# First attention of a fused block: queries and keys through memory in rounded parts, scores transposed by the matmul, exp read from PSUM

## The reference, cut to what matters

```python
qh = layernorm(heads(layernorm(x) @ Wq.T + bq), q_gamma, q_beta) * scale   # per head, 16 features
kh = layernorm(heads(ctx @ Wk.T + bk), k_gamma, k_beta)
attn = softmax(einsum('bhqd,bhkd->bhqk', qh, kh))                           # 77 keys
x = x + einsum('bhqk,bhkd->bhqd', attn, vh) @ Wp.T + bp
# next: router logits of layernorm(x), the two best of 8 experts
```

## Time and profile before

| | us |
|---|---|
| median of 3 runs (1414.25 to 1416.54) | 1415.62 |
| the profiled execution | 1416.21 |
| its span | 1414.3 |
| projections | 0 to 110.5 |
| first attention | 110.5 to 371.5 |
| everything behind it | 371.5 to 1414.3 |

### The profile page before, as it was taken

One profiled execution on the slowest core, in us unless ns is written; L12 is line 12 of the kernel. 1 busy time (PEld: TensorE's weight loads), 2 busy tenths in 40 slices (PEclk: granted clock), 3 DMA queues, 4 the chain that ended last, 5 costly groups with the idle time before them and its releaser, 6 DMA issues. The chain is left out here.

```text
span 1414.3 us, 29515 instructions
## 1 busy us (share of the span) xinstructions
PE 1286.1 (91%) x7733; PEld 1026.7 (73%) x7734; DVE 918.5 (65%) x2179; ACT 657.7 (47%) x1386; POOL 715.3 (51%) x903
## 2 busy tenths in 40 slices
PE   7997999999779999999998599857999999859998
PEld 4665777777448888888886477525888888747786
DVE  4784888888656777777776688692333333346665
ACT  2464777777325454544544477454333333221120
POOL 1223566565214655565554466306555555167775
PEclk9998999999799999999999699858999999979999
DMA  3118322222624555555554787535555556664443
GB/s 98 53 37 311 112 86 90 89 82 97 243 101 129 158 157 165 167 156 158 168 163 115 253 234 229 193 149 201 164 162 159 162 162 147 144 212 131 131 132 117
DMA packets 125980, 212.73 MB, mean 150 GB/s; under 512 B 17802, under 2 KB 92571, under 8 KB 122588
## 3 DMA queue, kind: packets, MB, share of 16 engines
q1 hardware_dynamic: 94276, 137.52, 31.5%
q0 software_dynamic: 20640, 56.39, 14.5%
q10 hardware_dynamic: 11000, 18.06, 3.4%
HBM read 148.03 MB, written 59.64 MB: 147 GB/s over the span
## 5 line engine op out<-in xcount | busy, mean ns | idle before, releaser
L1222 POOL DMA_INDIRECT xg<-t_xn,token x160 | 151.7, 948 | 154.6 <-PE psum L2120 70.6
L2196 POOL DMA_INDIRECT su_yg<-t_y,slot x128 | 122.8, 959 | 70.1 <-issue 38.1
L2132 PE MATMUL psum<-gu,m_xT 128*128 x640 | 153.0, 382 | 0.0
L2091 DVE TENSOR_TENSOR m_h<-psum,m_sg 128x256 f32<-128x256 f32 x80 | 33.9, 424 | 157.8 <-ACT m_sg L2070 157.8
L2132 PEld LDWEIGHTS psum<-gu,m_xT 128*128 128x128 f32 x640 | 116.6, 192 | 12.8
L1475 PE MATMUL psum<-w,m_xT_high 128*128 x284 | 119.0, 419 | 0.0
L1497 PE MATMUL psum<-m_both,m_hT_high 128*128 128x512 f32 x284 | 112.5, 418 | 1.4 <-DVE top_i L1441 1.3
L1475 PE MATMUL psum<-w_low,m_xT_high 128*128 x284 | 112.8, 397 | 0.0
L1475 PE MATMUL psum<-w,m_xT_low 128*128 x284 | 112.6, 397 | 0.0
L1348 POOL DMA_INDIRECT t_y<-top_v,dest x36 | 67.8, 1883 | 70.1 <-DVE top_v L1441 69.8
L1422 DVE TENSOR_TENSOR m_both<-w,m_both 128x1024 fp32r<-128x1024 f32 x71 | 87.0, 1225 | 14.1 <-ACT m_both L1390 10.9
(11 more groups left out here) (309 smaller groups left out, 3467.3 us busy)
## 6 DMA issues: line engine op xcount, KB each, us to landing
w<-in_w SPq DMA_DIRECT2D x71, 512.0 KB, 3.8
t_y<-m_y SPq DMA_DIRECT2D x80, 256.0 KB, 2.2
w<-in_w SPq DMA_DIRECT2D x8, 1024.0 KB, 11.3
t_x<-at_x SPq DMA_DIRECT2D x64, 128.0 KB, 2.0
t_w_low<-at_low ACTq DMA_DIRECT2D x64, 128.0 KB, 1.7
w_low<-t_w_low SPq DMA_DIRECT2D x8, 1024.0 KB, 13.3
at_yg<-t_y SPq DMA_DIRECT2D x32, 256.0 KB, 3.3
gu<-in_gu ACTq DMA_DIRECT2D x8, 1024.0 KB, 12.4
```

The lines of the kernel that those rows point to most:

```text
L1222: pool.indirect_dma_start(out=g.xg1[j % GB][:, k * D:(k + 1) * D], out_offset=None, in_=g.xn4, in_offset=bass.IndirectOffsetOnAxis(ap=g.to ...
L2132: last = pe.matmul(ps_gu[p][:, k * 2 * M1:(k + 1) * 2 * M1], xT[p][:, at:at + P], g.gu[:, bass.ds(ex[k] * (DC * 2 * M1) + c * 2 * M1, 2 * ...
L2196: pool.indirect_dma_start(out=yg[p][k][:, :], out_offset=None, in_=g.y1, in_offset=bass.IndirectOffsetOnAxis(ap=g.slot[:, at:at + 1], axis ...
```

## The change

Keys and queries no longer stay in SBUF. `affine` writes each result twice, once in full and once rounded to fp32r (`high`); GpSimd's `part` makes the difference (`low`); SyncE's `store` writes both parts to memory. Before each batch `load_queries_keys` brings them back in nine transfers, as tiles whose rows 0 to 95 are (high, high, low) of the queries and (high, low, high) of the keys, two heads to a tile, the keys in a block for each head. One fp32r matmul over 96 rows then gives the sum of the three products.

```diff
+    def store(self, sp, i):
+        for which, (rows, s_made) in enumerate(((self.high[p], self.s_out), (self.low[p], self.s_low))):
+            sp.wait_ge(s_made, i.n + 1)
+            for first, last in self.store_rows:      # keys: 1, queries: 4
+                sp.dma_start(self.stored[which](i.n, first, last), ...).then_inc(self.st[p], 16)
...
     def affine(self, act, i, s_passed):
+        wait(act, self.s_low, i.shift(-1).n)
+        wait(act, self.st[p], i.div(2).n * self.landed)
         wait_alone(act, self.s_t, i.n + 1, s_passed)
+        for out in (self.full, self.high):
+            last = act.activation(out[p], self.ps_t[:, 0:n], ACT.Identity, bias=self.beta, scale=self.gamma)
...
+def load_queries_keys(sp, g, b, slot):
+    for j, part in enumerate((0, 0, 1)):
+        sp.dma_start(g.q3[slot][32 * j:32 * j + 32, :]..., g.q_parts[part][:, b, :, :]).then_inc(landed, 16)
+    for j, part in enumerate((0, 1, 0)):
+        for a in range(2):
+            sp.dma_start(g.k3[slot][at:at + DH, :]..., g.k_parts[part]...).then_inc(landed, 16)
...
+            def step(s):                              # SyncE, projections
+                if i.within(NQP) and not (i.loop is None and i.off < 4):
+                    load_x(i)
+                if (at := piece(s, OUT + 1)) is not None:
+                    at[0].store(sp, at[1])
+                if s.off in PRELOAD:                  # steps 14, 16, 18, 20: batches 0 to 3
+                    load_queries_keys(sp, g, b, b)
```

```diff
 # TensorE
-                    for a in range(2):
-                        last = pe.matmul(ps_s[:, a, 0:HW], q_s[...], kblk[...])
+                    for i in range(HG // 2):
+                        last = pe.matmul(ps_s[...], g.q3[slot][0:96, ...128...], g.k3[slot][0:96, ...2 * LK...])
+                    for j in range(QUAD):
+                        last = pe.matmul(ps_st[0:LK, ...], g.k3[slot][0:98, ...LK...], g.q3[slot][0:98, ...SQ...])
+                    for a in range(2):
+                        last = pe.matmul(ps_m[:, a * P:(a + 1) * P], mx[...][:, a * HG:(a + 1) * HG], g.ident[:, :])
-                    for h in range(HG):
-                        last = pe.transpose(ps_tp[...], pr[p][:, h * LK:(h + 1) * LK], g.ident[:, :])
 # ScalarE
+                    act.activation(prT[p][0:LK, :]..., ps_st[0:LK, :, :], ACT.Exp)
+                    ln.apply_scalar(act, x1[p][:, :], xn[p][:, :], t)
+                    act.activation(mT[gr][96:96 + HG, :], ps_m, ACT.Copy).then_inc(mt_out, 1)
-                    act.activation(oraw[p][:, :], ps_raw, ACT.Copy).then_inc(raw_out, 1)
 # VectorE
+                    dve.tensor_copy(oraw[b.mod(2)][:, side * 4 * P:(side + 1) * 4 * P], ps_raw).then_inc(raw_out, 1)
-                    ln.apply(dve, x1[p][:, :], xn[p][:, :], t).then_inc(x_norm, 1)
 # SyncE, in this order in a step
+                    sp.wait_ge(mt_out, m.n + 1)       # even steps: two transfers with maxima
+                    expert_weights(e)                 # every eighth step
+                        load_queries_keys(sp, g, nxt.n, nxt.mod(QK_RING))   # every fourth step, until batch 15
+                    input_rows(t)
+                    sp.dma_start(g.w13_low_d[...], low[i.mod(4)][:, :])     # from ScalarE's queue
+                    # x1 and xn out; at step 12 also the 12 transfers for the next phase
-        T_RAW, T_N, T_O, T_WP, T_X, T_R = 4, 5, 6, 7, 9, 10
+        T_ST, T_PV = 5, 6
+        T_RAW, T_N, T_O, T_WP, T_INV, T_AP, T_X, T_R = 10, 12, 14, 15, 16, 17, 19, 20
```

More of the change, by code:

```diff
@@ L174, in __init__ @@
         self.eps, self.ps_p, self.ps_t = eps, ps_p, ps_t
+        n = 2 * DC * rows
+        at = [parts[:, i * n:(i + 1) * n] for i in range(6)]
+        self.full, self.high, self.low = at[0:2], *([a.bitcast(F32R) for a in at[i:i + 2]] for i in (2, 4))
+        self.stored, self.store_rows = stored, store_rows
+        self.landed = 2 * len(store_rows) * 16
         self.sq, self.n = ([sb(f"{name}_{n}{i}", [P, 2 * D]) for i in range(2)] for n in ("sq", "n"))
@@ new lines, in store @@
+    def store(self, sp, i):
+        p = i.mod(2)
+        for which, (rows, s_made) in enumerate(((self.high[p], self.s_out), (self.low[p], self.s_low))):
+            sp.wait_ge(s_made, i.n + 1)
+            for first, last in self.store_rows:
+                sp.dma_start(self.stored[which](i.n, first, last),
+                             rows[first:last, :].bitcast(F32).rearrange("p (c t) -> p c t", c=DC)).then_inc(self.st[p], 16)
+QK_LOADS, QK_RING = 9, 4
+Q_ROWS = [(i * 2 * DH, (i + 1) * 2 * DH) for i in range(P // (2 * DH))]
@@ L329, in _, with step @@
             pool.memset(g.v_all[:, :], 1.0).then_inc(s_v1, 1)
[L331 to L337, removed]
+            for slot in range(QK_RING):
+                pool.memset(g.k3[slot][0:96, :].bitcast(F32), 0.0).then_inc(s_zero, 1)
+            def step(s):
+                if (i := pair(s, X)) is not None:
+                    p = i.mod(2)
+                    wait_alone(pool, ln_mv, i.n + 1, passed[1])
+                    inverse_root(pool, rstd[p][:, :], mv[p][:, :].rearrange("p (a n) -> p a n", a=2)[:, :, 1],
+                                 g.minus_half[:, 0:2], ln_eps, ln_rstd, i)
+                if (at := piece(s, OUT)) is not None:
+                    at[0].part(pool, at[1])
+            steps(pool, FIRST, LAST, TOTAL, BODY, step)
         @block.vector
@@ L607, in _ @@
+            few(TOTAL, half)
             for p in range(2):
@@ new lines, in half @@
+                if v is not None:
+                    b, quad = v.div(4), v.mod(4)
+                    slot = b.mod(QK_RING)
+                    if quad % 2 == 0:
+                        pe.wait_ge(s_mr[quad // 2], (b.n + 1) * 32)
+                    wait(pe, exp_done, v.n)
+                    for j in range(QUAD):
+                        h = 2 * quad + j // 2
+                        last = pe.matmul(ps_st[0:LK, j // 2, j % 2 * SQ:(j % 2 + 1) * SQ],
+                                         g.k3[slot][0:98, (2 * h + j % 2) * LK:(2 * h + j % 2 + 1) * LK],
+                                         g.q3[slot][0:98, h * SQ:(h + 1) * SQ], start=True, stop=True)
+                    last.then_inc(st_mm, 1)
@@ L776, in half @@
+                m = max_rows(u)
+                if m is not None:
+                    pe.wait_ge(mx_ready, m.n * 2 + 2)
+                    wait(pe, mt_out, m.n)
                     for a in range(2):
-                        last = pe.matmul(ps_s[:, a, 0:HW], q_s[p][:, gr * P:(gr + 1) * P],
-                                         kblk[b.mod(2)][:, (2 * gr + a) * HW:(2 * gr + a + 1) * HW],
+                        last = pe.matmul(ps_m[:, a * P:(a + 1) * P], mx[m.mod(2)][:, a * HG:(a + 1) * HG], g.ident[:, :],
```

443 lines of the change are left out of this document (251 added, 192 removed).

## The result

The changed kernel takes 1446.28 us (median of 4 runs, 1435.50 to 1450.47), the kernel before 1416.08 in the same session: ratio 1.0203, 95% interval 1.0141 to 1.0266. It is 2.0% slower, where 1384 was forecast, and lies outside the range of 1360 to 1420. The profiled execution took 1450.25 us, one of the two longest of the four, with a span of 1448.4: projections to 150.5 (40.0 longer), attention to 404.15 (7.35 shorter instead of 63), the rest 1044.25 (1.45 longer).

A forecast was written before the change was run, and what follows sets the result against it. The prediction took TensorE to bound the first attention and SyncE's queue to bind the changed projections. From 1416.2 us it took 63 for the attention, added 30 for the projections and 1.2 for a meeting: 1384, range 1360 to 1420.

The forecast's parts named there:

- The attention: Attention stage: a tile on TensorE costs 5.48 us in place of 7.46, 63 us less over 32 tiles.
- Start and end: Attention outside its steady tiles: 6 us start, 4 stall, 10 last tiles' chain; 20, as the 22 now.
- step 12's stall: Attention, step 12: twelve more transfers pass ahead in SyncE's queue, one stall of about 4 us.
- Maxima scores: Attention: four fp32r matmuls of 154 columns a unit, 0.09 us each, 0.36 a unit; bounds 0.067 and 0.27.
- Transposed scores: Attention: four fp32r matmuls of 256 columns a unit, 4 x 0.112 = 0.45 us.
- Transposed maxima: Attention: two fp32 matmuls of 128 columns, 0.48 us a tile.
- hidden behind TensorE: Projections: ScalarE's second `affine` and GpSimd's difference, 41 and 33 of 48.5 us, add no time.
- Three steps of room: Attention: three steps (8 us) between maxima and transposed scores cover a landing of 1.9, at most 5.4 us.
- A: Attention: short fp32r matmuls run at the fp32 rate, giving 1422 us; chance 0.20.
- C: Projections: the stores hide, ending 3 us later instead of 30, giving 1357 us; chance 0.06.
- D: Attention: the maxima come late every time, 1.9 us for each of 32 tiles, giving 1445 us; chance 0.05.
- B: Attention: SyncE's queue binds there too, 18 us more, giving 1402 us; chance 0.14.

The follow-up runs named there:

- warm_units: Changed kernel plus 4 unread fp32 128x128 products in each of attention units 1 to 14; 1438.34 us.
- warm_proj: Changed kernel plus unread fp32 products in the projections, 5 behind each query pair and 40 at the end; 1448.53 us.
- late_loads: one_store with step 12's twelve loads issued as 17 pieces, one every second step from 14 on; 1433.85 us.
- max_fit: late_max with ScalarE's copy of the transposed outputs moved ahead of its two issues of the maxima; 1405.26 us, ratio to before 0.9929.
- one_store: Changed kernel with each half of a pair's queries stored in one transfer of 128 partitions instead of four of 32; 1426.19 us.
- pause: max_fit with one added TensorE wait, ahead of unit 28's scores, for a residual store to land; 1408.63 us.
- late_max: late_loads with the maxima's two transfers a tile issued by ScalarE instead of SyncE; 1419.70 us, ratio to before 1.0021.

## Why the prediction was wrong

**The clock, the step that failed.** Every duration in "The attention" came from rows at a clock of 1.00, and "Start and end" had 6 us for the start, 4 for the stall and 10 for the last chain. TensorE's idle time did come out at 22.0, in part by luck: 3.2 before step 12's stall, 4.6 for it and 9.0 at the end, and 5.3 in the middle that had been put at nothing. But the 64 units were priced at full clock throughout, and some 39.9 us came from the low one. The rows to ask about were there: 110.50 to 371.50 at 0.96, the end at 0.79. In the kernel before, the stage had 247.88 - 239 = 9 us of it. warm_units and warm_proj show one source, the first units' mix; late_loads and max_fit the other, waits for the maxima, with some 12 us (231.6 - 219.3). The Trainium skill ("TensorE: Matmul & The Clock Gate", HAM oscillation — how this bites in real kernels) tells of waits for a DMA that take the clock down so that its return is paid again each time. late_loads agrees, with prices from some 4 to some 26 us at half clock behind waits of 2.80 to 2.89. The same page (What's actually happening) puts the cost of warming up, one ramp, below 1% of a typical span. Here the slow first units and the falls behind waits came to some 39.9 of 1448 us together, 2.8%, and the measurement decides.

**The tile.** 5.99 instead of 5.48, 16.3 us in all. Maxima scores: 0.50 a unit where 0.36 was taken, so 0.125 for a matmul of 154 columns and not the router's 0.09. Transposed scores: 0.48 and 0.57 where 0.45 was. Transposed maxima 0.53 (0.48), products 0.55 (0.56), the rest 2.31 (2.26). The bounds 0.067 and 0.27 held.

**The projections.** Mechanism right (the queue full from 66 on, the meeting when SyncE is through), size off: 171 x 0.49 from 66.4 in place of 172 x 0.44 from 64.6. A second step was wrong and hidden by this one: that the second `affine` and the difference are "hidden behind TensorE". With the queue out of the way (one_store) a pair takes 4.1 us on average (66.84 to 128.94), not 3.1, and the projections end near 130. `affine` now takes ScalarE 1.45 us a pair instead of 0.78, and TensorE's next transposes wait for it (5.8 us in three waits). That this chain sets the pace is argued from the rows; TensorE's clock of 0.66 between 100 and 110 has a part in it too.

**Engines and room.** VectorE and ScalarE fit under TensorE, as said. "Three steps of room" for the maxima held in 27 tiles of 32; step 12's stall was forecast at 4 us and was 4.56. The room was counted with a landing of 1.9 to 5.4 us; behind bulk loads of the same queue the maxima of one_store landed 6.8 us after their issue (182.82 to 189.6). That such a wait also costs the clock was not in it.

**The rivals.** A is refuted by the 0.125 us. C is refuted by the queue, and by one_store, where the queue is no longer the bound and the end is 131, not 113. D happened five times, not each time: 9.1 us. B did not bind: TensorE is busy for 96% of the time from 233.70 to 365.70. None of the four was the case that came; the clock was no rival.

**Open.** Why the clock came back some 4 us after one wait (9.22 us in one_store, 2.80 in late_loads) and 26 after another (2.88), why waits of 1.88 and 1.57 us in the changed kernel (at 269.54 and 295.73) left it at 1.00, and why it stayed at 0.51 for 33.8 us without a gap, is not settled; only that the mix with wider fp32 products brought it up in 8 us. The split of the 39.9 us, some 12 behind waits and the rest in the first units and the end, is an estimate from two kernels, one execution each.

## What to carry to other kernels

A matmul saved is worth its time at the clock that its stretch is granted: look up that clock in the windows of the profile, and ask whether the new mix or a new wait lowers it. When data go through memory instead of staying in SBUF, count every transfer of the queue that issues them, and also the chain for one item behind that queue. Don't issue a small transfer that TensorE waits for behind bulk loads: give it another engine's queue, at a place in that engine's list where nothing waits.

## What was not expected of the hardware

- A wait of TensorE of 2.29 us brought the granted clock from 1.00 to 0.50 for some 6 us (pause), one of 2.80 for some 4 and one of 2.88 for some 26 (late_loads), one of 9.22 for some 4 (one_store).
- The granted clock was 0.51 over 33.8 us in which TensorE had no gap, the 1.2 GHz level but for the end, and was at the 2.4 GHz level 8 us into the stage with 4 unread fp32 products of 128x128 a unit.
- Moving two 4 KB transfers a tile to ScalarE's queue removed TensorE's waits for them (late_loads 9.4 us in 5 waits, late_max 0.5 in one) with all other bytes as before. The Trainium skill ("DMA: Bandwidth & Descriptors", Issuing engines are not separate DMA queues) says that transfers of several engines interleave on the same DMA engines and that a second issuing engine saves only issue time. No run here shows the interleaving itself; the saving was larger than issue time (1.2 us a tile), since the small transfers no longer came behind the bulk ones of their own queue.
- Back to back, a store of 32 partitions holds SyncE's queue for about as long as one of 128: 0.48 us from start to start in the kernel after (four from 139.94 to 141.86), 0.51 in one_store (98.70 to 99.21).
